# Two attention stages of a fused kernel: scores of two batches matmul by matmul on two halves of the rows, weighing in two parts

## The chip, the cores and the metric

The kernel runs as one program on one core of a Trainium2 chip. The time is device microseconds (us) of the execution, the median of several. The engines are named as in the profile: PE (TensorE, matmul), PEld (its weight loads), DVE (VectorE), ACT (ScalarE), POOL (GpSimd), SP (SyncE, here the issuer of most DMAs).

## The reference, cut to what matters

The program is a chain of eight layers on an input of 32 batches x 256 tokens x 128 features. Two of them are softmax attention with 16 heads of 8 features; everything else is untouched by the change.

```
# L2 attention (stage h2), causal
scores = einsum('bqhd,bkhd->bhqk', Q, K) / sqrt(8)
scores = where(causal, scores, -inf); attn = softmax(scores, -1)
out = einsum('bhqk,bkhd->bqhd', attn, V).reshape(...) @ W_o
# L3 attention inside the last FFN (stage h3), not causal, the same with biases
```

## The kernel before

`attend` runs twice: tag h2 with `causal=True`, tag h3 with `causal=False`. Both loop over 32 batches, in a hardware loop whose body is four batches (`SLOTS`), with three batches before it and four behind. Q and K arrive from DRAM as bf16 parts: 48 rows (`KR`, six parts of eight features) and 3 more (`KM` = 51) that hold, on the K side, ones and, on the Q side, first zeros and later the negated row maximum in three bf16 parts. The tiles `sq[u]` and `sk[u]` have 128 partitions x 16 heads x 256 tokens; partitions 51 to 127 are zero, and every score matmul contracts over all 128.

One pipelined `step(b, ...)` interleaves, head by head, three batches:

- `scores(b, u, h)` (L2105): K^T Q of head h of batch b, with the maximum already subtracted through the extra rows, into one of three PSUM banks (`ps_2`); two matmuls. ACT takes the exponential (`weights`, L2194) into `pt`.
- `max_scores(b + 2, ..., h)` (L2090): Q^T K of head h of the batch after the next, into one of two PSUM banks (`ps_1`); two matmuls. DVE takes its maximum (`maximum`, L2021) into `mx`.
- in h2 each of these matmuls is half or fully above the diagonal, so it has 128 or 256 columns, and is followed by a matmul of 128 columns that adds the mask (L2101, L2116).
- `weigh` (L2120), once for each group of four heads (`HG`): 8 matmuls in fp32 of V against `pt`, which write four column strips of 32 partitions; an fp32 matmul is two instructions for PE, so the trace has 16.
- around them: `turn_sums`, `turn_max`, `turn_out` (transposes) and `project_out`, on PE; `keep_sums` and the copies `oT`, `mpart` on ACT; `norm` (L2032: a reciprocal and a product), `mrest` (L2051), the residual add (L2056), `count` and `nm` (L2069) on DVE.

The order of all this is written out by hand in `step` of each engine: g runs over four groups, j over the four heads of a group. What waits for what is a semaphore count: `max_scores` of head h waits until DVE is done with head h - 2 (same bank), `scores` of head h until ACT is done with head h - 3. `project_out(b - 1)` stands on PE behind `scores` of head 12; it waits for ACT's copy `oT` (L2234), which stands on ACT behind `keep_sums` of the group and the exponential of head 11; and `keep_sums` waits for `weigh` (semaphore `pv`).

## Time and profile before

| | |
|---|---|
| median of 3 runs | 3908.71 us (3904.9 to 3912.76) |
| the profiled execution | 3900.78 us, its span 3898.9 us |
| mean granted clock of PE | 0.855 |
| busy | PE 2895.4 us (74%), DVE 2436.3 us (62%), ACT 1764.7 us (45%), POOL 594.0 us (15%) |
| first to last matmul of the scores of h2 and h3 | 1971 us to 2493 us, and 2977 us to 3507 us |

The profile is one execution. "Busy" is the time in which an engine had an instruction under way. A matmul's row lasts from its start to its result, so matmuls of a stream overlap: the pace is the distance of their starts. A row "x2, 0.39" is two matmuls merged. Idle time is shown in brackets with what ended it.

### The profile page before, as it was taken

To read this page: it belongs to the slowest core of one execution; us is meant where nothing else is said; L and a number is where in the kernel's file an instruction comes from. 1 tells how busy PE (TensorE), PEld (TensorE's weight loads), DVE (VectorE), ACT (ScalarE), POOL (GpSimd) and SP (SyncE) were. 2 spreads that over 40 slices of the span, in tenths; PEclk is the share of its full clock that TensorE was granted. 3 is DMA by queue.
4 is the path that set the end of the run, shared out by engine and by line. 5 is a ranking of instruction groups with operands and counts; after the bars stand their busy time and mean duration, and the time that the engine had idled before them with its cause. 6 is when DMAs were issued, how large, how long until landed. Compare 5 with 4: busy or idle time off the path is not lost. (4 is left out here: it accounts for less than half of the span.)

```text
span 3898.9 us, 82957 instructions
## 1 busy us (share of the span) xinstructions
PE 2895.4 (74%) x22031; PEld 2090.7 (54%) x22031; DVE 2436.3 (62%) x6570; ACT 1764.7 (45%) x4634; POOL 594.0 (15%) x911
## 2 busy tenths in 40 slices
PE   0444976999898688992469999868894999994061
PEld 0233563459787458991257777765452555554060
DVE  5852767238786435775667777557446777767167
ACT  5320632334353355661346666621122666672243
POOL 0000000000000586770000000000000000000773
PEclk9977968999997899996889999886556999995595
DMA  9069200100001111224865555000255555420123
GB/s 223 5 132 250 65 6 8 33 24 0 0 1 49 37 46 57 68 66 117 283 72 67 66 64 67 13 1 0 77 188 88 64 63 63 63 34 31 47 78 101
DMA packets 348796, 264.84 MB, mean 68 GB/s; under 512 B 20504, under 2 KB 331208, under 8 KB 348040
## 3 DMA queue, kind: packets, MB, share of 16 engines
q1 hardware_dynamic: 326944, 227.12, 29.0%
q0 software_dynamic: 12928, 26.70, 2.0%
q10 hardware_dynamic: 8704, 8.39, 0.7%
q8 instruction: 101, 1.65, 0.2%
q14 instruction: 119, 0.97, 0.1%
HBM read 145.70 MB, written 114.86 MB: 67 GB/s over the span
## 5 line engine op out<-in xcount | busy, mean ns | idle before, releaser
L2098 PE MATMUL h_ps<-h_sk,h_sq 128*128 128x256 bf16 (+1 forms) x2048 | 407.1, 267 | 113.1 <-DMA h_vb<-v_ones 95.9
L2113 PE MATMUL h_ps<-h_sq,h_sk 128*128 128x256 bf16 (+1 forms) x2048 | 393.9, 261 | 41.5 <-issue 21.2
L2030 DVE TENSOR_REDUCE h_mx<-h_ps 128x2 f32<-128x512 f32 x512 | 333.7, 684 | 114.7 <-PE h_ps L2098 96.7
L2204 ACT ACTIVATE h_pt<-h_ps 128x512 f32<-128x512 f32 x512 | 286.9, 593 | 100.1 <-PE h_ps L2113 89.7
L1446 POOL TENSOR_TENSOR idle<-idle 128x1 f32<-128x1 f32 x400 | 101.3, 253 | 1439.0 <-ACT e_row L1510 1368.4
L2098 PEld LDWEIGHTS h_ps<-h_sk,h_sq 128*128 128x128 bf16 x2048 | 174.7, 99 | 249.2 <-issue 120.3
L2201 ACT ACTIVATE h_pt<-h_ps 128x256 f32<-128x256 f32 x512 | 196.3, 383 | 115.3 <-PE h_ps L2116 113.4
L2128 PE MATMUL h_ps_o<-h_pt,h_vb 128*9 128x256 f32 (+1 forms) x4096 | 243.2, 355 | 0.9 <-ACT h_pt L2204 0.5
L2113 PEld LDWEIGHTS h_ps<-h_sq,h_sk 128*128 128x128 bf16 x2048 | 198.7, 99 | 77.8 <-issue 27.1
L1645 POOL DMA_INDIRECT results<-e_y,e_ykey x208 | 221.6, 1065 | 70.0 <-issue 67.0
L2080 POOL TENSOR_TENSOR h_mpart<-h_mrest,h_mpart 16x256 bf16<-16x256 f32 x64 | 42.3, 661 | 1242.7 <-ACT h_mpart L2230 1242.7
L2027 DVE TENSOR_REDUCE h_mx<-h_ps 128x1 f32<-128x128 f32 x512 | 147.2, 287 | 131.2 <-PE h_ps L2101 127.9
L2028 DVE TENSOR_REDUCE h_mx<-h_ps 128x1 f32<-128x256 f32 x512 | 211.6, 413 | 0.0
L1694 ACT ACTIVATE e_hid<-e_ps_h,e_wt 128x128 f32<-128x128 f32 x688 | 201.5, 367 | 7.4 <-PE e_ps_h L1668 3.0
L2101 PE MATMUL h_ps<-h_mskb 128*128 128x128 bf16 x1024 | 200.6, 222 | 0.0
L1603 DVE TENSOR_SCALAR e_wt<-w 128x1156 f32 (+1 forms) x208 | 142.8, 687 | 88.7 <-DVE e_y L1634 69.7
L1668 PE MATMUL e_ps_h<-e_hT,e_wt 128*128 128x128 f32 x1376 | 197.3, 283 | 0.3 <-ACT e_hT L1689 0.3
L1495 POOL DMA_INDIRECT sorted_rows<-e_row,e_key x192 | 189.3, 986 | 35.4 <-issue 18.8
L1676 PE MATMUL e_ps_o<-e_wt,e_hid 128*128 128x128 f32 x1376 | 190.0, 277 | 0.1
L1668 PEld LDWEIGHTS e_ps_h<-e_hT,e_wt 128*128 128x128 f32 x1376 | 174.2, 196 | 8.3 <-issue 2.3
L1661 PE MATMUL e_ps_t<-pack,e_xt 128*128 128x128 f32 x208 | 60.8, 294 | 158.7 <-DMA e_xt<-sorted_rows 158.3
L1676 PEld LDWEIGHTS e_ps_o<-e_wt,e_hid 128*128 128x128 f32 x1376 | 172.8, 194 | 0.4 <-issue 0.3
(410 smaller groups left out, 6878.9 us busy)
## 6 DMA issues: line engine op xcount, KB each, us to landing
h_sq<-q_stack SPq DMA_DIRECT2D x64, 384.0 KB
h_sk<-k_stack SPq DMA_DIRECT2D x64, 384.0 KB
sorted_rows<-pad SPq DMA_DIRECT2D x26, 520.0 KB, 10.5
e_xt<-sorted_rows SPq DMA_DIRECT2D x52, 260.0 KB, 2.8
e_got<-results SPq DMA_DIRECT2D x48, 256.0 KB, 4.6
q_stack<-p_parts SPq DMA_DIRECT2D x32, 384.0 KB, 2.6
k_stack<-p_parts SPq DMA_DIRECT2D x32, 384.0 KB, 3.3
v_ones<-p_v SPq DMA_DIRECT2D x32, 288.0 KB, 2.6
```

Source lines behind the costliest of these rows:

```text
L1645: gp.indirect_dma_start(ys[:, :], bass.IndirectOffsetOnAxis(ap=key[m // 4][:, m % 4:m % 4 + 1], axis=0), y[m % 4][:, :], None).then_inc(sc ...
L1668: pe.matmul(ps_h[:, k, 0:P], wt[j % 4][:, f * P:(f + 1) * P], hT[j % 4][:, :], start=True, stop=True).then_inc(e_h.sem, 1)
L1676: ins = pe.matmul(o, hid_t[m][:, f, :], wt[m][:, f_dim + f * D:f_dim + (f + 1) * D], start=(f == 0), stop=(f == nf - 1))
L1694: act.activation(hid_t[j % 4][:, f, :], ps_h[:, (j * nf + f) % 4, 0:P], func, bias=wt[j % 4][:, o_b1 + f:o_b1 + f + 1]).then_inc(e_a.sem, 1)
L2028: dve.tensor_reduce(mx[:, h, 1:2], sv[:, 1, :], AX, ALU.max).then_inc(s["mx"].sem, 1)
L2030: dve.tensor_reduce(mx[:, h, :], sv, AX, ALU.max).then_inc(s["mx"].sem, 1)
L2098: ins = pe.matmul(o, sq[u][:, h, q * P:(q + 1) * P], sk[u][:, h, 0:nk], start=True, stop=not causal)
L2101: ins = pe.matmul(o[:, q * P:nk], mskb[:, 0:P], mskb[:, P:2 * P], start=False, stop=True)
L2113: ins = pe.matmul(o[:, q0:], sk[u][:, h, t * P:(t + 1) * P], sq[u][:, h, q0:], start=True, stop=not causal)
L2128: ins = pe.matmul(o, vb[u][:, t, HG * g + j, :], pt[g % 2][:, j, t, q0:], start=(t == 0), stop=(t == TPB - 1), skip_group_check=True)
L2201: act.activation(to[:, 0, :], sv[:, 0, :], ACT.Exp, scale=scale)
L2204: act.activation(to, sv, ACT.Exp, scale=scale).then_inc(s["ex"].sem, 1)
```

## The change

Heads are split by parity. `sq` and `sk` have 8 places instead of 16; an even head lies on partitions 0 to 63 (51 used, the rest zeros), an odd head on 64 to 127. Each score matmul contracts over 64 partitions. On PE the two functions become one, `both(n)`, that waits for all it needs and then issues, in turn, matmul 0 of the scores of head n, matmul 0 of the maximum scores of head n ^ 1 (the other half of the partitions), matmul 1 and matmul 1. In h2 the four mask matmuls, which still contract over 128 partitions, come behind these four. DVE takes the maxima in the order 1, 0, 3, 2, ... `weigh` is issued in two parts, key tile 0 behind `both` of the third head of a group, key tile 1 behind that of the fourth; `turn_sums` moves ahead of `both` of the fourth head, `turn_max` behind the second part of `weigh`. DVE does `norm` behind the maximum of the fourth head, not ahead of it. Head 15 of the scores uses bank 1 instead of 0, so head 0 of the next batch needn't wait for it. Loads of a batch are 7 DMAs instead of 4 (half the size each, but for V), the maxima come in by 2 DMAs instead of 1.

The diff, with the unchanged part of long passages cut:

```diff
-                ("min", 16), ("s2", NH), ("ex", NH), ("pv", 4), ("ev", 4), ("tu", 4), ("rec", 4), ("on", 4), ("ot", 1),
+                ("min", 32), ("s2", NH), ("ex", NH), ("pv", 4), ("ev", 4), ("tu", 4), ("rec", 4), ("on", 4), ("ot", 1),
-            loaded=[SlotSignal(pool, f"{t}_loaded{u}", 64, u, 4) for u in range(4)]) for t in ("h2", "h3")}
+            loaded=[SlotSignal(pool, f"{t}_loaded{u}", 112, u, 4) for u in range(4)]) for t in ("h2", "h3")}
...
-                sq = [sb(f"{tag}_sq{u}", [P, NH, SEQ], BF16, stack=st) for u in range(SLOTS)]
-                sk = [sb(f"{tag}_sk{u}", [P, NH, SEQ], BF16, stack=st) for u in range(SLOTS)]
-                zrow = sb(f"{tag}_zrow", [KM - KR, NH, SEQ], BF16, stack=st)
+                sq = [sb(f"{tag}_sq{u}", [P, NH // 2, SEQ], BF16, stack=st) for u in range(SLOTS)]
+                sk = [sb(f"{tag}_sk{u}", [P, NH // 2, SEQ], BF16, stack=st) for u in range(SLOTS)]
+                zrow = sb(f"{tag}_zrow", [KM - KR, NH // 2, SEQ], BF16, stack=st)
...
+                def bank_of(h):
+
+                    return h % 3 if h < NH - 1 else 1
...
-                            sp.dma_start(sk[u][KR:KM, :, :], ones_rows).then_inc(ones_in[n_att], 16)
+                            for half in (0, 64):
+                                sp.dma_start(sk[u][half + KR:half + KM, :, :], ones_rows[:, 0:NH // 2, :]
+                                             ).then_inc(ones_in[n_att], 16)
...
-                            sp.dma_start(sq[u][0:KR, :, :], q_stack.rearrange("h e a t -> (e a) h t")[:, :, cols]
-                                         ).then_inc(up, 16)
-                            sp.dma_start(sk[u][0:KR, :, :], k_stack.rearrange("h e a t -> (e a) h t")[:, :, cols]
-                                         ).then_inc(up, 16)
-                            sp.dma_start(sq[u][KR:KM, :, :], zrow[:, :, :]).then_inc(up, 16)
+                            for odd in range(2):
+                                rows = slice(64 * odd, 64 * odd + KR)
+                                sp.dma_start(sq[u][rows, :, :], q_stack.rearrange("(h o) e a t -> o (e a) h t", o=2)
+                                             [odd, :, :, cols]).then_inc(up, 16)
+                                sp.dma_start(sq[u][64 * odd + KR:64 * odd + KM, :, :], zrow[:, :, :]).then_inc(up, 16)
+                                sp.dma_start(sk[u][rows, :, :], k_stack.rearrange("(h o) e a t -> o (e a) h t", o=2)
+                                             [odd, :, :, cols]).then_inc(up, 16)
...
-                                sp.dma_start(sq[ahead(u, r, 1)[0]][KR:KM, :, :], m_parts).then_inc(s["min"].sem, 16)
+                                for odd in range(2):
+                                    sp.dma_start(sq[ahead(u, r, 1)[0]][64 * odd + KR:64 * odd + KM, :, :],
+                                                 m_parts.rearrange("a (h o) t -> o a h t", o=2)[odd]
...
-                        def maximum(b, h):
-                            dve.wait_ge(*at("s1", b, h + 1))
-                            if h == 0:
+                        def maximum(b, n):
+                            h = n ^ 1
+                            dve.wait_ge(*at("s1", b, n + 1))
...
+                                    if first:
+                                        maximum(b + 2, HG * g + j)
                                     if j == 3 and g < 2 and tail:
                                         norm(b - 1, g + 2)
                                     if j == 3 and g >= 2 and body:
                                         norm(b, g - 2)
-                                    if first:
-                                        maximum(b + 2, HG * g + j)
...
-                        pe.wait_ge(ones_in[n_att], 16 * SLOTS)
-
-                        def max_scores(b, u, r, h):
...
-                        def weigh(b, u, g):
+                        pe.wait_ge(ones_in[n_att], 2 * 16 * SLOTS)
+
+                        def max_score(u, h, q):
+                            rows = slice(64 * (h % 2), 64 * (h % 2) + 64)
+                            nk = (q + 1) * P if causal else SEQ
+                            o = ps_1[:, h % 2, q * SEQ:q * SEQ + nk]
+
+                            return pe.matmul(o, sq[u][rows, h // 2, q * P:(q + 1) * P], sk[u][rows, h // 2, 0:nk],
+                                             start=(q == 0 or not causal), stop=not causal, skip_group_check=causal)
+
+                        def max_mask(h, q):
+                            o = ps_1[:, h % 2, q * SEQ + q * P:q * SEQ + (q + 1) * P]
+                            return pe.matmul(o, mskb[:, 0:P], mskb[:, P:2 * P], start=False, stop=True, skip_group_check=True)
+
+                        def score(u, h, t):
+                            rows = slice(64 * (h % 2), 64 * (h % 2) + 64)
+                            q0 = t * P if causal else 0
+                            o = ps_2[:, bank_of(h), t * SEQ:(t + 1) * SEQ]
+                            return pe.matmul(o[:, q0:], sk[u][rows, h // 2, t * P:(t + 1) * P], sq[u][rows, h // 2, q0:],
+                                             start=(t == 0 or not causal), stop=not causal, skip_group_check=causal)
+
+                        def score_mask(h, t):
+                            o = ps_2[:, bank_of(h), t * SEQ + t * P:t * SEQ + (t + 1) * P]
+                            return pe.matmul(o, mskb[:, 0:P], mskb[:, 2 * P:3 * P], start=False, stop=True, skip_group_check=True)
+
+                        def weigh(b, u, g, t):
 
                             pe.wait_ge(*at("ex", b, HG * (g + 1)))
                             pe.wait_ge(*at("ev", b, g))
-                            for t in range(TPB):
-                                q0 = t * P if causal else 0
-                                for j in range(HG):
-                                    o = ps_o[32 * j:32 * j + VW, 0, q0:SEQ]
-                                    ins = pe.matmul(o, vb[u][:, t, HG * g + j, :], pt[g % 2][:, j, t, q0:], start=(t == 0),
-                                                    stop=(t == TPB - 1), skip_group_check=True)
-                            ins.then_inc(s["pv"].sem, 1)
+                            q0 = t * P if causal else 0
+                            for j in range(HG):
+                                o = ps_o[32 * j:32 * j + VW, 0, q0:SEQ]
+                                ins = pe.matmul(o, vb[u][:, t, HG * g + j, :], pt[g % 2][:, j, t, q0:], start=(t == 0),
+                                                stop=(t == TPB - 1), skip_group_check=True)
+                            if t == TPB - 1:
+                                ins.then_inc(s["pv"].sem, 1)
...
-                            later = ahead(u, r, 2)
+                            later, r_later = ahead(u, r, 2)
+
+                            def both(n):
+
+                                if body:
+                                    if n == 0:
+                                        pe.wait_ge(*at("min", b, 32))
+                                    pe.wait_ge(*at("ex", b, n - 2 if 1 < n < NH - 1 else (-3, 0)[n] if n < 2 else n - 1))
+                                if first:
+                                    if n == 0:
+                                        pe.wait_ge(*s["loaded"][later].now(r_later, 112))
+                                    pe.wait_ge(*at("mx", b + 2, n - 1))
+                                for k in range(TPB):
+                                    if body:
+                                        ins = score(u, n, k)
+                                        if k == TPB - 1 and not causal:
+                                            ins.then_inc(s["s2"].sem, 1)
+                                    if first:
+                                        ins = max_score(later, n ^ 1, k)
+                                        if k == TPB - 1 and not causal:
+                                            ins.then_inc(s["s1"].sem, 1)
+                                if body and causal:
+                                    score_mask(n, 0)
+                                    score_mask(n, 1).then_inc(s["s2"].sem, 1)
+                                if first and causal:
+                                    max_mask(n ^ 1, 0)
+                                    max_mask(n ^ 1, 1).then_inc(s["s1"].sem, 1)
+
                             for g in range(GROUPS):
                                 for j in range(HG):
-                                    if body:
-                                        scores(b, u, HG * g + j)
+                                    if j == 3:
+                                        if g < 2 and tail:
+                                            turn_sums(b - 1, g + 2)
+                                        if g >= 2 and body:
+                                            turn_sums(b, g - 2)
+                                    both(HG * g + j)
                                     if j == 1 and g == 2 and tail:
                                         turn_out(b - 1, turn)
                                     if j == 0 and g == 3 and tail:
                                         project_out(b - 1)
-                                    if j == 2:
+                                    if j >= 2:
                                         if g and body:
-                                            weigh(b, u, g - 1)
+                                            weigh(b, u, g - 1, j - 2)
                                         if not g and tail:
-                                            weigh(b - 1, (u - 1) % SLOTS, GROUPS - 1)
-                                    if j == 3:
-                                        if g < 2 and tail:
-                                            turn_sums(b - 1, g + 2)
-                                        if g == 0 and turn:
-                                            turn_max(b + 1)
-                                        if g >= 2 and body:
-                                            turn_sums(b, g - 2)
-                                    if first:
-                                        max_scores(b + 2, *later, HG * g + j)
+                                            weigh(b - 1, (u - 1) % SLOTS, GROUPS - 1, j - 2)
+                                    if j == 3 and g == 0 and turn:
+                                        turn_max(b + 1)
...
-                            sv = ps_2[:, h % 3, :].rearrange("p (t q) -> p t q", t=TPB)
+                            sv = ps_2[:, bank_of(h), :].rearrange("p (t q) -> p t q", t=TPB)```

On PE in h3, around `project_out` (L2161 and L2162 of before, L2166 and L2167 of the change). Before, L2098 is the maximum, L2113 the scores, L2128 the weighing, L2136 `turn_sums`:

```order
L2128 MATMUL h_ps_o<-h_pt,h_vb 9x256 x8
L2094 REGISTER_ALU
L2098 MATMUL h_ps<-h_sk,h_sq 128x256 x2
L2109 REGISTER_ALU
L2113 MATMUL h_ps<-h_sq,h_sk 128x256 x2
L2134 REGISTER_ALU
L2136 MATMUL h_ps_s<-pack,h_sums 128x128 x2
L2094 REGISTER_ALU
L2098 MATMUL h_ps<-h_sk,h_sq 128x256 x2
L2109 REGISTER_ALU
L2113 MATMUL h_ps<-h_sq,h_sk 128x256 x2
L2157 REGISTER_ALU
```

With the change, L2118 is the scores, L2107 the maximum, L2132 the weighing, L2141 `turn_sums`:

```order
L2132 MATMUL h_ps_o<-h_pt,h_vb 9x256 x4
L2139 REGISTER_ALU
L2141 MATMUL h_ps_s<-pack,h_sums 128x128 x2
...
L2132 MATMUL h_ps_o<-h_pt,h_vb 9x256 x4
L2178 REGISTER_ALU
L2182 REGISTER_ALU
L2118 MATMUL h_ps<-h_sq,h_sk 128x256
L2107 MATMUL h_ps<-h_sk,h_sq 128x256
L2118 MATMUL h_ps<-h_sq,h_sk 128x256
L2107 MATMUL h_ps<-h_sk,h_sq 128x256
L2162 REGISTER_ALU
```

Between the end of the weighing and the wait of `project_out` (the last row) there were the maximum of two heads and the scores of two; now there is one `both`.

On PE in h2, one head before and one head with the change (L2101, L2116 and L2112, L2123 are masks):

```order
L2094 REGISTER_ALU
L2098 MATMUL h_ps<-h_sk,h_sq 128x128
L2101 MATMUL h_ps<-h_mskb 128x128
L2098 MATMUL h_ps<-h_sk,h_sq 128x256
L2101 MATMUL h_ps<-h_mskb 128x128
L2109 REGISTER_ALU
L2113 MATMUL h_ps<-h_sq,h_sk 128x256
L2116 MATMUL h_ps<-h_mskb 128x128
L2113 MATMUL h_ps<-h_sq,h_sk 128x128
L2116 MATMUL h_ps<-h_mskb 128x128
```

```order
L2182 REGISTER_ALU
L2118 MATMUL h_ps<-h_sq,h_sk 128x256
L2107 MATMUL h_ps<-h_sk,h_sq 128x128
L2118 MATMUL h_ps<-h_sq,h_sk 128x128
L2107 MATMUL h_ps<-h_sk,h_sq 128x256
L2123 MATMUL h_ps<-h_mskb 128x128 x2
L2112 MATMUL h_ps<-h_mskb 128x128 x2
```

The count of matmuls is the same; the masks moved from between to behind, so each head now goes once from matmuls on half the rows to matmuls on all of them and back.

## Rows read from the trace of the kernel before

**Rows 1.** Windows: PE, PEld, DVE, ACT, POOL busy us (count), clock, DMA share, GB/s.
```profile
2100.00:2200.00 100.00, 92.01 (x1296) 72.60 (x1296) 74.44 (x283) 68.74 (x244) 3.97 (x6) 0.99 0.49 65
3100.00:3200.00 100.00, 94.61 (x922) 57.00 (x922) 78.44 (x182) 69.70 (x145) 3.96 (x6) 1.00 0.53 66
```
**Rows 2.** Timeline of DVE, once a batch: start us, us; h2, then h3.
```profile
2246.41 0.18 DVE L2069 TENSOR_SCALAR h_nm<-h_mx 128x32 f32<-128x32 f32 x1
2261.58 0.17 DVE L2069 TENSOR_SCALAR h_nm<-h_mx 128x32 f32<-128x32 f32 x1
...
3193.46 0.18 DVE L2069 TENSOR_SCALAR h_nm<-h_mx 128x32 f32<-128x32 f32 x1
3209.57 0.18 DVE L2069 TENSOR_SCALAR h_nm<-h_mx 128x32 f32<-128x32 f32 x1
```
**Rows 3.** Timeline of PE in h2: the maximum scores of two heads in a row.
```profile
2252.34 0.22 PE L2098 MATMUL h_ps<-h_sk,h_sq 128*128 128x128 bf16 x1
...
2252.90 0.22 PE L2098 MATMUL h_ps<-h_sk,h_sq 128*128 128x128 bf16 x1
```
**Rows 4.** Timeline of PE in h2, around one weighing.
```profile
2250.64 0.22 PE L2116 MATMUL h_ps<-h_mskb 128*128 128x128 bf16 x1
2250.78 0.84 PE L2128 MATMUL h_ps_o<-h_pt,h_vb 128*9 128x256 f32 x16
2251.56 0.23 PE L2098 MATMUL h_ps<-h_sk,h_sq 128*128 128x128 bf16 x1
```
**Rows 5.** Timeline of PE in h3: a weighing, one head, sums turned.
```profile
3201.09 1.05 PE L2128 MATMUL h_ps_o<-h_pt,h_vb 128*9 128x256 f32 x16
3202.08 0.39 PE L2098 MATMUL h_ps<-h_sk,h_sq 128*128 128x256 bf16 x2
3202.31 0.38 PE L2113 MATMUL h_ps<-h_sq,h_sk 128*128 128x256 bf16 x2
3202.52 0.38 PE L2136 MATMUL h_ps_s<-pack,h_sums 128*128 128x128 f32 x2
```
**Rows 6.** Timeline of PE in h3: `project_out`, 1-row and 128-row matmuls in turn.
```profile
3203.65 0.48 PE L2161 MATMUL h_ps_m<-pack 1*128 1x128 f32 x2 [0.31 <-ACT h_oT L2234]
...
3204.28 0.28 PE L2162 MATMUL h_ps_m<-pack,h_oT 128*128 128x128 f32 x1
3204.48 0.37 PE L2161 MATMUL h_ps_m<-pack 1*128 1x128 f32 x1
```
**Rows 7.** Timeline of DVE and PE in h2: last mask of a maximum, and its reduction.
```profile
2251.79 0.22 PE L2101 MATMUL h_ps<-h_mskb 128*128 128x128 bf16 x1
2252.05 0.29 DVE L2027 TENSOR_REDUCE h_mx<-h_ps 128x1 f32<-128x128 f32 x1 [0.49 <-PE h_ps L2101]
2252.25 0.41 DVE L2028 TENSOR_REDUCE h_mx<-h_ps 128x1 f32<-128x256 f32 x1
```
**Rows 8.** Timeline of DVE in h3, and of PE where it waited for DVE.
```profile
3202.51 0.69 DVE L2030 TENSOR_REDUCE h_mx<-h_ps 128x2 f32<-128x512 f32 x1 [0.82 <-PE h_ps L2098]
...
3209.18 0.48 DVE L321 BATCH_NORM_STATS2 bn<-x  x2
...
3210.01 1.95 DVE L2030 TENSOR_REDUCE h_mx<-h_ps 128x2 f32<-128x512 f32 x3 [0.27 <-DVE h_nm L2069]
3211.88 0.20 DVE L2037 RECIPROCAL h_rec<-h_ps_s 128x8 f32<-128x8 f32 x1
...
3212.25 1.87 DVE L2030 TENSOR_REDUCE h_mx<-h_ps 128x2 f32<-128x512 f32 x3
3212.99 0.39 PE L2098 MATMUL h_ps<-h_sk,h_sq 128*128 128x256 bf16 x2 [0.23 <-DVE h_mx L2030]
```
**Rows 9.** Timeline of ACT in h3: the sums kept behind the weighing.
```profile
3202.29 0.38 ACT L2209 ACTIVATE h_sums<-h_ps_o 128x256 f32<-128x256 f32 x1 [0.49 <-PE h_ps_o L2128]
```
**Rows 10.** Timeline of PE in h2 where the hardware loop turns.
```profile
2262.78 0.28 PE L2113 MATMUL h_ps<-h_sq,h_sk 128*128 128x256 bf16 x1 [2.29 <-issue]
```
**Rows 11.** One line's instructions, min/median/max ns: the clearing of `sq`.
```profile
L2014 DVE MEMSET h_sq<- x8: 1765/1765/1765, 1938.9 to 2959.4; 128x2048 uint32 x8
```

More of the change, by code:

```diff
@@ L2003, in step @@
                                 sp.wait_ge(*at("mout", b + 1, 16))
-                                sp.dma_start(sq[ahead(u, r, 1)[0]][KR:KM, :, :], m_parts).then_inc(s["min"].sem, 16)
+                                for odd in range(2):
+                                    sp.dma_start(sq[ahead(u, r, 1)[0]][64 * odd + KR:64 * odd + KM, :, :],
+                                                 m_parts.rearrange("a (h o) t -> o a h t", o=2)[odd]
+                                                 ).then_inc(s["min"].sem, 16)
                         for b in range(SLOTS):
@@ L2087, in _ @@
                         pe.wait_ge(chained, k_set)
-                        pe.wait_ge(ones_in[n_att], 16 * SLOTS)
-                        def max_scores(b, u, r, h):
-                            if h == 0:
-                                pe.wait_ge(*s["loaded"][u].now(r, 64))
-                            pe.wait_ge(*at("mx", b, h - 1))
-                            for q in range(TPB):
-                                nk = (q + 1) * P if causal else SEQ
-                                o = ps_1[:, h % 2, q * SEQ:q * SEQ + nk]
-                                ins = pe.matmul(o, sq[u][:, h, q * P:(q + 1) * P], sk[u][:, h, 0:nk],
-                                                start=True, stop=not causal)
-                                if causal:
-                                    ins = pe.matmul(o[:, q * P:nk], mskb[:, 0:P], mskb[:, P:2 * P],
-                                                    start=False, stop=True)
-                            ins.then_inc(s["s1"].sem, 1)
@@ L2105, in scores @@
-                        def scores(b, u, h):
-                            if h == 0:
-                                pe.wait_ge(*at("min", b, 16))
-                            pe.wait_ge(*at("ex", b, h - 2 if h else 0))
-                            for t in range(TPB):
-                                q0 = t * P if causal else 0
-                                o = ps_2[:, h % 3, t * SEQ:(t + 1) * SEQ]
-                                ins = pe.matmul(o[:, q0:], sk[u][:, h, t * P:(t + 1) * P], sq[u][:, h, q0:],
-                                                start=True, stop=not causal)
-                                if causal:
-                                    ins = pe.matmul(o[:, q0:q0 + P], mskb[:, 0:P], mskb[:, 2 * P:3 * P],
-                                                    start=False, stop=True)
-                            ins.then_inc(s["s2"].sem, 1)
@@ L2122, in weigh @@
+                        def score_mask(h, t):
+                            o = ps_2[:, bank_of(h), t * SEQ + t * P:t * SEQ + (t + 1) * P]
+                            return pe.matmul(o, mskb[:, 0:P], mskb[:, 2 * P:3 * P], start=False, stop=True, skip_group_check=True)
+                        def weigh(b, u, g, t):
                             pe.wait_ge(*at("ex", b, HG * (g + 1)))
                             pe.wait_ge(*at("ev", b, g))
-                            for t in range(TPB):
-                                q0 = t * P if causal else 0
-                                for j in range(HG):
-                                    o = ps_o[32 * j:32 * j + VW, 0, q0:SEQ]
-                                    ins = pe.matmul(o, vb[u][:, t, HG * g + j, :], pt[g % 2][:, j, t, q0:], start=(t == 0),
-                                                    stop=(t == TPB - 1), skip_group_check=True)
@@ L2197, in weights @@
                             act.wait_ge(*at("pv", b, g - 1))
-                            sv = ps_2[:, h % 3, :].rearrange("p (t q) -> p t q", t=TPB)
+                            sv = ps_2[:, bank_of(h), :].rearrange("p (t q) -> p t q", t=TPB)
                             to = pt[g % 2][:, j]
```

1 line of the change is left out of this document (added).

## The prediction

> **What bounds the kernel now.** The kernel is a chain of layers, and the change touches two of them, so I read these two alone: the windows first, then the pace of a batch, then single instructions in time. In the windows [rows 1] PE is busy 92% in h2 and 95% in h3, DVE 74% and 78%, ACT below both, the clock is at its upper level of 2.4 GHz (0.99 and 1.00), DMA at half. The batch takes 15.2 us in h2 (2246.41 to 2261.58) and 16.1 us in h3 [rows 2]. So PE is the first suspect, in h2 above all: the maximum scores of a head begin 0.56 us behind those of the head before [rows 3], 16 x 0.56 = 9.0 of the 15.2 us; a weighing takes 2250.64 + 0.06 to 2251.56, 0.86 us [rows 4], four make 3.4; transposes and the output projection fill the rest. In h3 four score matmuls of 256 columns take 0.44 us (3202.08 to 3202.52) [rows 5], 7.0 us a batch; the rest of the 16.1 is weighing, projection and waits between PE and DVE, as the 0.82 us in which DVE stood still behind a weighing [rows 8].
>
> **What the change gives.** Two matmuls on different halves of the rows should run beside each other. That matmuls on different parts of the array do so this trace shows for column strips only: the 16 of a weighing, of 0.38 us each, start and stream within 0.99 us [rows 5]. Taken for row halves: in h3 a head costs PE 0.22 instead of 0.44 us (two streams of 256 columns), in h2 0.22 instead of 0.32 before masks (0.56 with them, at 0.06 for each mask). If nothing overlaps, both stay; that is the other end.
>
> **What it costs on PE: changes of shape.** Where PE goes from matmuls on all of the array to matmuls on a part, the trace has a gap. In h2 the last mask starts at 2250.64 and streams 0.06, the weighing starts at 2250.78: 0.08 lost [rows 4]. `project_out` of h3 has it for rows, not columns: behind a 128-row matmul at 3204.28 that streams 0.11 the 1-row matmul starts at 3204.48, 0.09 late, and its own row lasts 0.37 instead of 0.28 because its weights could not be loaded ahead [rows 6]. I take 0.10 for each change of shape, 0.15 into an fp32 transpose; the ends are 0 (if halves of 64 rows don't count as a shape of their own) and 0.20. The Trainium skill (TensorEngine Tiling, Key Properties) says that changing the tiling mode drains TensorE, while changing the tile within a mode doesn't; it gives no duration. The rows above agree; by that rule each `both` of h2 pays twice.
>
> In h2 a head then takes 0.22 + 0.10 + 4 x 0.055 + 0.10 = 0.64 us instead of 0.56. The overlap saves 0.10 and the two changes cost 0.20.
>
> **h2, one group of four heads.** Times from the start of `both` of its third head, each step from the durations above. `both` to 0.54; first half of the weighing 0.64 to 1.07 (four strips of two streams of 256 columns, 0.43); sums turned to 1.44; `both` of the fourth head 1.54 to 2.08; second half of the weighing 2.18 to 2.39 (128 columns); `both` of the next head 2.49 to 3.03. DVE starts 0.26 behind the last mask and works 0.61 [rows 7], so a maximum starts 0.75 behind its `both`: the fourth from 2.29 to 2.90. Then `norm`, now behind it: the reciprocal starts 0.08 before the end (1.95 us from 3210.01, reciprocal at 3211.88) and the next maximum 0.37 later [rows 8]: 3.19. The next maximum starts at 3.24 and ends at 3.85. PE needs 0.06 to go on behind DVE (second maximum of the 1.87 us from 3212.25 still runs; the first ends at 3212.93, PE at 3212.99) [rows 8]. So the third head of the next group starts at **3.91**. This is the new wait: before, `max_scores` alone waited for DVE and the scores of the next head ran meanwhile; now both wait, and the signal to DVE comes only behind four masks. Group 0 has `turn_max` as well (0.37): 4.28. The last group has `count` and `nm` behind `norm`, 0.83 from 3209.18 to 3210.01 [rows 8], which the slack of DVE hid before: 2.29 + 0.53 + 0.37 + 0.83 + 0.67 = 4.69.
>
> **`project_out`.** ACT's chain: end of the weighing, sums kept (3202.29 [rows 9]), exponential of head 11, copy `oT`, projection at 3203.65 [rows 6]. From the end of the weighing's streams (3202.08 - 0.10) that is 1.67 us. Before, PE had two heads' maxima and scores to do meanwhile and stood idle 0.31 [rows 6]. Now the weighing ends one `both` later and only one `both` lies between, so PE and, behind it, DVE stand. In h2: 2.39 + 1.67 = 4.06, projection 0.6 (four fp32 matmuls; half of h3's at most 0.8), next `both` 4.76 to 5.30, third head at 5.40. The batch: 4.28 + 3.91 + 5.40 + 4.69 = 18.3 instead of 15.2, **+3.1 us**; x 31 full batches = +96.
>
> **h3, the same.** Here DVE sets the pace: a maximum 0.62 behind the last ((1.87 - 0.68) / 2 is 0.60, (1.95 - 0.68) / 2 is 0.63) [rows 8], ready 0.45 behind `both` (3202.08 to 3202.51 for two matmuls 0.11 apart [rows 5, 8]). From the first maximum of a group at 0: `both` of the third head at 0.74, weighing half, sums turned, three gaps, `both` of the fourth at 0.74 + 0.22 + 0.10 + 0.43 + 0.10 + 0.27 + 0.10 = 1.96; its maximum at 2.41, 0.55 later than DVE could; `norm`; next group at 2.41 + 0.60 + 0.37 = 3.38. Group 0 has `turn_max`: 3.63. With the projection (1.6; half of it takes 3203.65 to 3204.48 [rows 6]): first maximum of the last group at 3.63 + 3.38 + 3.38 = 10.39, weighing ended at 9.72, projection 11.39 to 12.99, `both` of head 13 at 13.09, of 14 at 13.31, of 15 at 14.53, maximum 15 at 14.98, then 0.60 + 0.37 + 0.83: **16.8 instead of 16.1**, x 31 = +22. PE has 0.22 x 16 = 3.5 us less to stream in a batch; it goes into gaps (some 25 a batch, 2.5 us) and waits.
>
> **Smaller parts.** Eight clearings a stage at 1.765 us become half as long [rows 11], and so does that of `zrow`: 8 us ahead of all work of each stage, -16. At the turn of the hardware loop in h2 PE stands 2.29 us for "issue" [rows 10], once in four batches, 7 times; a PE that runs less far ahead of its waits hides part of it: -10, between 0 and -30. The DMAs: the same bytes in seven issues instead of four, 3 batches ahead; nothing waits there while a batch takes 15 us. Two DMAs for the maxima instead of one: some 0.3 us on a chain with microseconds to spare; nothing.
>
> **Sum.** +96 + 22 - 16 - 10 = +92. The profiled execution (span 3898.9, 3900.8 with what lies around) would go to 3993; the median lies 7.9 higher, so 3908.7 + 92 = **4000 us**.
>
> **Rivals.**
> *Halves of the rows change without a gap (faster).* For it: no row of this trace has a 64-row matmul. Against: rows 6. Then in h2 a head takes 0.44, a group 0.44 + 0.43 + 0.22, `both` at 1.09, its maximum at 1.74, the next at 2.64, third head at 3.31; with projection (1.74 + 1.67 + 0.6 = 4.01) 4.45, last 4.09: 15.2, nothing won or lost, since the wait for ACT and the delayed signal stay. In h3 `both` of the fourth at 1.61, group 3.04, last group as above: 15.5, -0.6 x 31 = -19. With -16 and -10: 3864. It decides from a gap below 0.03.
> *Halves do not overlap.* The Trainium skill (TensorE: Matmul & The Clock Gate, Part 3) has matmuls on different row groups start about 4 ns apart; no row here shows it. Without overlap each `both` takes 0.22 more in h3 and 0.10 in h2; two lie in the chain of each group: +1.8 and about +1 a batch, +87: 4087.
> *Half a gap*, 0.05: between the first rival and the forecast, 3930; with more of the waits hidden than I find, no change.
>
> **Chances.** Forecast (3945 to 4060) 0.60; no gap or waits that hide better 0.25; half a gap 0.08; no overlap 0.07. The range 3860 to 4060 holds the first three but for the tail of the second. Within 0.2% (3901 to 3916), which is about what a measurement of this kernel can tell from no change, I put 0.06; faster 0.25; slower 0.69.
>
> **What would show it.** In the profile after: the `nm` rows 18.3 us apart in h2 and 16.8 in h3 (step by step: below 15.2 in h2 and the forecast has failed); in h2 0.10 us between the last row matmul and the first mask beyond the stream, and again behind the masks; PE idle over 1 us ahead of the projection; DVE idle some 2 us behind it; score and maximum matmuls that start in pairs. Masks that follow without a gap would bring down the h2 term, pairs 0.11 us apart would raise both.

## Result and profile after

| | before | after |
|---|---|---|
| median of 4 runs each | 3906.81 us | 4041.5 us (4028.94 to 4045.2) |
| ratio, 95% interval | 1 | 1.0339 (1.0311 to 1.0367) |
| the profiled execution, its span | 3900.78, 3898.9 us | 4028.94, 4027.1 us |
| mean granted clock | 0.855 | 0.844 |

Slower by 3.4%, where the prediction said slower, 4000 us, at most 4060. The forecast was +92 us in a profiled execution; the two spans are 128.2 apart. The first and last start of the score matmuls say where. For each kernel the first row is h2 and the second h3. Before:

```profile
L2113 PE MATMUL h_ps<-h_sq,h_sk x1024: 217/272/421, 1993.8 to 2492.5; 128*128 128x256 bf16 x171
L2113 PE MATMUL h_ps<-h_sq,h_sk x1024: 269/273/421, 3000.3 to 3506.5; 128*128 128x256 bf16 x171
```

After:

```profile
L2118 PE MATMUL h_ps<-h_sq,h_sk x1024: 213/278/393, 1989.6 to 2579.0; 64*128 64x256 bf16 x171
L2118 PE MATMUL h_ps<-h_sq,h_sk x1024: 266/279/418, 3060.9 to 3633.6; 64*128 64x256 bf16 x171
L2025 DVE MEMSET h_sq<- x8: 912/912/912, 1943.3 to 3024.1; 128x1024 uint32 x8
```

h2 went from 498.7 to 589.4 (**+90.7**), h3 from 506.2 to 572.7 (**+66.5**); ahead of h2 -4.2, between the two stages 507.8 to 481.9 (-25.9), behind h3 +1.1. The last row is the halved clearing [rows 11]. From the first clearing to the first matmul of a maximum, a stage now takes 12 us less: 22.1 us instead of 34.5 ahead of h2 (1942.1 to 1964.2, and 1936.7 to 1971.2), and 22.2 instead of 33.8 ahead of h3. Ahead of h2 that is partly hidden, since the layers before it ended 5 us later. The other 14 between the stages lie in layers that the change does not touch.

Windows of after over both stages (columns as [rows 1]), then one batch of h3 at a lower clock, one at the full clock; last, for after and for before, what follows the last `nm` of h3:

```profile
2000.00:2520.00 520.00, 457.92 (x5762) 223.66 (x5760) 335.22 (x1245) 274.64 (x1081) 17.83 (x27) 0.97 0.35 55
3070.00:3590.00 520.00, 435.91 (x4292) 158.96 (x4295) 370.39 (x840) 301.68 (x669) 19.60 (x30) 0.90 0.35 55
...
3294.50:3314.00 19.50, 16.52 (x148) 5.46 (x148) 12.78 (x30) 10.02 (x24) 0.66 (x1) 0.82 0.33 52
3332.03:3348.65 16.62, 13.59 (x148) 5.22 (x148) 12.68 (x30) 10.47 (x25) 0.66 (x1) 1.00 0.40 61
...
3598.10:3633.60 35.50, 32.20 (x220) 10.46 (x220) 4.99 (x22) 19.29 (x43) 0.66 (x1) 0.67 0.01 3
3483.70:3506.50 22.80, 20.91 (x222) 11.57 (x211) 4.75 (x20) 18.35 (x42) 0.66 (x1) 1.00 0.02 5
```

PE is busy 88% in h2 and 84% in h3, where it was 92 and 95 [rows 1]. In h3 the clock is 0.90 where it was 1.00: a batch takes 16.62 us at the full clock (16.1 before [rows 2]) and mostly 17.5 to 19.6 where it fell; only about a third of the batches had it whole.

Timeline of PE in h2 after, one head and the projection:

```profile
2300.02 0.28 PE L2118 MATMUL h_ps<-h_sq,h_sk 64*128 64x256 bf16 x1
2300.02 0.34 PE L2107 MATMUL h_ps<-h_sk,h_sq 64*128 64x128 bf16 x2
2300.14 0.22 PE L2118 MATMUL h_ps<-h_sq,h_sk 64*128 64x128 bf16 x1
2300.29 0.28 PE L2123 MATMUL h_ps<-h_mskb 128*128 128x128 bf16 x2
2300.41 0.27 PE L2112 MATMUL h_ps<-h_mskb 128*128 128x128 bf16 x2
2301.39 0.71 PE L2167 MATMUL h_ps_m<-pack,h_oT 128*128 128x128 f32 x4 [0.70 <-ACT h_oT L2263]
```

The two streams of the two halves start together. The pair streams 384 columns on either half (0.16 us), the mask starts 0.27 behind: 0.11 lost at the change of shape. A head takes 0.60 us (2226.42 to 2227.02), 0.56 before [rows 3].

Timeline of PE, DVE and ACT in h3 after, a weighing in two parts and the projection:

```profile
3332.99 0.28 PE L2118 MATMUL h_ps<-h_sq,h_sk 64*128 64x256 bf16 x1 [0.35 <-DVE h_mx L2042]
3332.99 0.28 PE L2107 MATMUL h_ps<-h_sk,h_sq 64*128 64x256 bf16 x1
...
3333.11 0.27 PE L2107 MATMUL h_ps<-h_sk,h_sq 64*128 64x256 bf16 x1
3333.31 0.62 PE L2132 MATMUL h_ps_o<-h_pt,h_vb 128*9 128x256 f32 x8
3333.86 0.44 PE L2141 MATMUL h_ps_s<-pack,h_sums 128*128 128x128 f32 x2
3334.23 0.28 PE L2118 MATMUL h_ps<-h_sq,h_sk 64*128 64x256 bf16 x1
...
3343.59 0.48 PE L2166 MATMUL h_ps_m<-pack 1*128 1x128 f32 x2 [1.02 <-ACT h_oT L2263]
```

```profile
3334.69 0.69 DVE L2042 TENSOR_REDUCE h_mx<-h_ps 128x2 f32<-128x512 f32 x1 [0.55 <-PE h_ps L2107]
...
3345.72 0.69 DVE L2042 TENSOR_REDUCE h_mx<-h_ps 128x2 f32<-128x512 f32 x1 [2.20 <-PE h_ps L2107]
```

```profile
3345.68 1.08 ACT L2233 ACTIVATE h_pt<-h_ps 128x512 f32<-128x512 f32 x2 [1.66 <-PE h_ps L2118]
```

Those are the predicted waits: DVE 0.55 behind the first half of a weighing (0.24 in the group in which it also does `mrest`), PE 1.02 ahead of the projection (0.31 before [rows 6]), and behind the projection DVE 2.20 and ACT 1.66.

### The profile page after: what moved, and what is told of

Read it like the earlier page. It is cut to its first block and busy times, and to the rows that moved or that the text cites. A ratio compares the mean times of both kernels' runs of the same rounds, so it can differ in the third digit from the quotient of the medians.

```text
span 4027.1 us, 83705 instructions
## 1 busy us (share of the span) xinstructions
PE 2957.0 (73%) x22031; PEld 1858.7 (46%) x22031; DVE 2432.7 (60%) x6570; ACT 1708.8 (42%) x4634; POOL 594.4 (15%) x911
## 5 line engine op out<-in xcount | busy, mean ns | idle before, releaser
L2118 PE MATMUL h_ps<-h_sq,h_sk 64*128 64x256 bf16 (+1 forms) x2048 | 379.5, 276 | 99.8 <-DVE h_mx L2042 28.4
L2107 PE MATMUL h_ps<-h_sk,h_sq 64*128 64x256 bf16 (+1 forms) x2048 | 390.6, 281 | 73.3 <-DMA h_vb<-v_ones 69.2
L2042 DVE TENSOR_REDUCE h_mx<-h_ps 128x2 f32<-128x512 f32 x512 | 337.5, 685 | 161.8 <-PE h_ps L2107 142.9
L2132 PE MATMUL h_ps_o<-h_pt,h_vb 128*9 128x256 f32 (+1 forms) x4096 | 313.8, 381 | 1.9 <-ACT h_pt L2233 1.0
L2233 ACT ACTIVATE h_pt<-h_ps 128x512 f32<-128x512 f32 x512 | 280.9, 588 | 74.9 <-PE h_ps L2118 72.2
L2118 PEld LDWEIGHTS h_ps<-h_sq,h_sk 64*128 64x128 bf16 x2048 | 121.0, 96 | 318.5 <-issue 134.5
L2238 ACT ACTIVATE h_sums<-h_ps_o 128x256 f32<-128x256 f32 x256 | 98.1, 383 | 371.3 <-PE h_ps_o L2132 371.3
L2107 PEld LDWEIGHTS h_ps<-h_sk,h_sq 64*128 64x128 bf16 x2048 | 122.6, 97 | 97.4 <-issue 71.0
```

Source lines behind the costliest of these rows:

```text
L2042: dve.tensor_reduce(mx[:, h, :], sv, AX, ALU.max).then_inc(s["mx"].sem, 1)
L2107: return pe.matmul(o, sq[u][rows, h // 2, q * P:(q + 1) * P], sk[u][rows, h // 2, 0:nk], start=(q == 0 or not causal), stop=not causal, sk ...
L2118: return pe.matmul(o[:, q0:], sk[u][rows, h // 2, t * P:(t + 1) * P], sq[u][rows, h // 2, q0:], start=(t == 0 or not causal), stop=not cau ...
L2132: ins = pe.matmul(o, vb[u][:, t, HG * g + j, :], pt[g % 2][:, j, t, q0:], start=(t == 0), stop=(t == TPB - 1), skip_group_check=True)
L2233: act.activation(to, sv, ACT.Exp, scale=scale).then_inc(s["ex"].sem, 1)
```

## Experiments

Ratios are to the kernel before on the same chip; e9 to e11 ran on another, where before takes 3945.6 us (3903.1 and 3902.8 for the others). The extra time of that chip lies ahead of h2 (in e11 the first matmul of a maximum starts at 2025.9, before at 1971.2), so batches can be compared. The table gives the batch at the full clock, and clock and PE busy share in 2000:2450 (h2) and 3100:3450 (h3); where a stage starts later the window does too, 2050:2500 for h2 of e9 to e11 and 3435:3785 for h3 of e2. Below, "less than after" goes by the medians. By the ratios, each good to 0.2 to 0.4%, e3 lies 33 us under after, e4 40, e6 8 and e7 57, and e5 lies 21 over it; so e6 can't be told from after by its time.

| run | ratio (95%) | h2 batch, clock, busy | h3 batch, clock, busy |
|---|---|---|---|
| before | 1 | 15.1, 0.98, 93% | 16.1, 1.00, 95% |
| after | 1.0339 | 17.65, 0.97, 88% | 16.62, 0.89, 84% |
| e1_full_rows | 1.0394 (1.0355 to 1.0432) | 17.52, 0.98, 88% | 18.13, 0.96, 89% |
| e2_same_half | 1.1738 (1.1702 to 1.1775) | 19.6, 0.62, 97% | 18.4 to 18.8, 0.67, 92% |
| e3_mask_half | 1.0255 (1.0224 to 1.0286) | 15.40, 0.89, 79% | as after, 0.91, 84% |
| e4_project_later | 1.0237 (1.0201 to 1.0272) | 17.05, 0.97, 90% | 16.34, 0.94, 85% |
| e5_weigh_whole | 1.0393 (1.0349 to 1.0436) | 17.27, 0.96, 87% | 17.12, 0.88, 79% |
| e6_project_last | 1.0319 (1.0282 to 1.0356) | 16.97, 0.95, 91% | 16.35, 0.90, 84% |
| e7_last_and_mask_half | 1.0193 (1.0155 to 1.0231) | 15.4, 0.92, 79% | as e6, 0.91, 84% |
| e8_before_project_last | 0.9964 (0.9946 to 0.9982) | 15.1, 0.98, 92% | 15.83, 1.00, 95% |
| e9_joined_only | 1.0223 (1.0198 to 1.0248) | 16.2, 0.96, 89% | 17.31, 1.00, 89% |
| e10_split_only | 1.0186 (1.0163 to 1.0209) | 16.4, 0.99, 93% | 17.39, 1.00, 93% |
| e11_before_project_mid | 1.0029 (1.0011 to 1.0047) | 15.1, 0.98, 93% | 16.44, 1.00, 94% |

**What do the halves give, what does the order cost?** e1_full_rows is the change with full-row tiles and the four DMAs of before:

```diff
-                            rows = slice(64 * (h % 2), 64 * (h % 2) + 64)
+                            rows = slice(0, P)
```

> The changed kernel with its order of work, but the tiles, loads and score matmuls of before: all score and maximum matmuls contract over 128 partitions, so nothing overlaps and nothing changes shape but the weighing and the projection. Theory (the changes of shape cost 0.10 us each, the overlap gives 0.10 a head in h2 and 0.22 in h3, the order of work makes the waits): a head of h2 goes from 0.61 to about 0.55 us and the batch from 17.65 to 16.9 us; a batch of h3 from 16.6 at the upper clock to 17.5 or 18, with a steadier clock since PE streams more; in all 4020 to 4070 us, within 1% of the changed kernel, so still well above before: the order by itself is slower. Rival (the new order is harmless, the half rows do the damage): back to before but for the missing overlap, 3900 to 3930 us.

4057.28 us, as expected, though with 17.5 us a batch in h2 and not 16.9. At the full clock the new order alone costs 2.4 us a batch in h2 and 2.0 in h3. On top, the halves add 0.1 in h2 (overlap against two changes of shape) and take 1.5 off in h3. So on full rows the order alone costs as much in h2 as the whole change, where I had put more on the shapes; and what the halves save in h3 the clock gives back (0.96 to 0.89).

**Is the overlap real?** e2_same_half: the maximum scores of head n, on the same half as its scores.

```diff
-                                        ins = max_score(later, n ^ 1, k)
+                                        ins = max_score(later, n, k)
```

> The changed kernel with the maximum scores of head n beside the scores of head n, both on the same half of the partitions, instead of head n ^ 1 on the other: no two matmuls can overlap, everything else stays. Theory (halves overlap almost fully): the starts of score and maximum matmuls are no longer in pairs but 0.11 us apart, h3 gains 0.4 to 0.5 us in each group of four heads (+1.6 to +2 a batch), h2 +0.1 to 0.2 in each group; in all +60 to +90 us over the changed kernel, 4100 to 4130. Rival (the pairs in the trace are only records, the streams are serial in the array): within 10 us of the changed kernel.

4573.56 us (five runs, 4505.54 to 4584.14; the profile is the fastest), over 440 beyond both expectations. Timeline of PE in h2, with its row behind a turn of the hardware loop; then windows: short ones at either clock, one batch at the full clock, and the whole stretch at the lower one:

```profile
2114.79 0.28 PE L2118 MATMUL h_ps<-h_sq,h_sk 64*128 64x256 bf16 x1
2114.91 0.22 PE L2107 MATMUL h_ps<-h_sk,h_sq 64*128 64x128 bf16 x1
2114.96 0.22 PE L2118 MATMUL h_ps<-h_sq,h_sk 64*128 64x128 bf16 x1
2115.02 0.27 PE L2107 MATMUL h_ps<-h_sk,h_sq 64*128 64x256 bf16 x1
...
2129.11 0.28 PE L2118 MATMUL h_ps<-h_sq,h_sk 64*128 64x256 bf16 x1 [3.07 <-issue]
```

```profile
2112.00:2117.00 5.00, 5.00 (x59) 2.86 (x58) 3.31 (x14) 2.95 (x13) 0.00 (x0) 1.00 0.77 137
2132.00:2157.00 25.00, 24.99 (x170) 11.92 (x167) 9.62 (x34) 8.55 (x32) 0.66 (x1) 0.50 0.26 42
...
2107.60:2127.20 19.60, 17.81 (x200) 9.77 (x200) 12.40 (x47) 9.94 (x39) 0.66 (x1) 1.00 0.35 54
2130.40:2212.10 81.70, 81.60 (x542) 39.05 (x542) 33.01 (x117) 27.52 (x103) 1.98 (x3) 0.50 0.24 38
```

On one half the matmuls follow one another (0.12, 0.05, 0.06 us apart), so the overlap of after is real. At the full clock a batch of h3 takes 18.4 to 18.8 us, 1.8 to 2.2 over after, as expected; one of h2 takes 19.6, 2.0 over after instead of 0.4 to 0.8. What was not foreseen is the clock. It falls behind the 3.07 us in which PE stands at the turn of the hardware loop, and then stays at 0.50, the 1.2 GHz level, for 82 us in which PE was busy all but 0.1 us. In after, too, the clock of h2 falls behind the turns (23.1 us a batch at 0.85), but there it comes back within the batch.

**What do the changes of shape cost in h2?** e3_mask_half puts the masks on the half of their head: 64 rows, each row of the weights serving two neighbouring queries or keys by factors of 1 and 2^-80 against -2^40 and -2^120. In h2 then only the weighing and the transposes change the shape.

```diff
-                            return pe.matmul(o, mskb[:, 0:P], mskb[:, P:2 * P], start=False, stop=True, skip_group_check=True)
+                            rows = slice(64 * (h % 2), 64 * (h % 2) + 64)
+                            return pe.matmul(o, mskb[rows, 0:P], mskb[rows, P:2 * P], start=False, stop=True, skip_group_check=True)
```

> The changed kernel with causal masks that contract over the 64 partitions of their head's half (each row of the mask matmul serves two tokens, with weights 1 and 2^-80 against -2^40 and -2^120), issued in pairs like the scores: no change of shape within a head, and masks that overlap too. Theory (two changes of shape at 0.10 us in each head are the loss in h2): a head of h2 takes 0.35 to 0.40 us instead of 0.61, the batch about 16.0 instead of 17.65 us, in all 45 to 60 us less than the changed kernel, 3980 to 3995; h3 is untouched. Rival (h2 is slower because both kinds of scores now wait for both engines, PE's own time hardly matters): less than 15 us.

3996.45 us, 45 less than after. PE in h2:

```profile
2265.06 0.28 PE L2119 MATMUL h_ps<-h_sq,h_sk 64*128 64x256 bf16 x1
...
2265.24 0.22 PE L2113 MATMUL h_ps<-h_mskb 64*128 64x128 bf16 x1
2265.24 0.22 PE L2125 MATMUL h_ps<-h_mskb 64*128 64x128 bf16 x1
...
2265.54 0.28 PE L2119 MATMUL h_ps<-h_sq,h_sk 64*128 64x256 bf16 x1
```

The mask follows 0.18 behind instead of 0.27, and two masks run beside each other. So the edit takes two things off a head, two changes of shape (0.22) and half of the masks' streams (0.11), and no run parts them. At the full clock the batch takes 15.4 us (16.0 expected), 2.2 less than after, which would be 70 us; but most batches took 16 to 19 us, at a clock of 0.89 (0.97 in after).

**The waits around projection and weighing.** e4_project_later has the projection one head later (`j == 1`), e5_weigh_whole both parts of the weighing behind the third head, e6_project_last the projection and DVE's add at the step's end, e7_last_and_mask_half is e6 with e3's masks.

```diff
-                                    if j == 0 and g == 3 and tail:
+                                    if j == 1 and g == 3 and tail:
```

> The changed kernel with the output projection one head later on PE (behind head 13, not 12). Theory (PE stands because ACT's copy oT comes 1.67 us behind the weighing): the idle time before the projection falls from 1.02 us in h3 and 0.70 in h2 by one head's work, 0.3 and 0.6; DVE gets one more maximum to do, but the projection itself, 1.6 us in h3, still stands in DVE's way: 0.25 us a batch less in h3, 0.5 in h2, in all 15 to 30 us less. Rival (the projection's place doesn't matter, PE has slack there): within 5 us.

> The changed kernel with both parts of a weighing behind the third head of a group, as before the change, everything else as changed. Theory (two chains: DVE waits for the work between two heads' matmuls, ACT's copy oT waits for the end of the weighing): the fourth head's maximum comes 0.3 to 0.4 us later in each group, but ACT's chain starts 1.2 us earlier, so PE's idle time before the projection (1.02 us in h3, 0.70 in h2) goes; the two about cancel, within 20 us of the changed kernel. Rival (splitting the weighing is the main loss of the new order, through its extra change of shape and the late signal to ACT): 50 us or more less.

> The changed kernel with the output projection at the very end of a step on PE (behind the last part of the weighing of the last group), and on DVE the residual add and its statistics behind nm, at the end as well. Theory (the wait for oT and the projection itself in front of head 13 are a main part of the new order's loss): PE's idle time before the projection and the 2.20 us in which DVE stands there go, but the residual add now waits for the projection at the end: about 1.1 us a batch less in h3 and 0.9 in h2, 55 to 70 us less than the changed kernel, 3970 to 3990. Rival (it is only moved): within 20 us of the kernel with the projection one head later, 3975 to 4010, with DVE idle as long at the step's end.

> The projection at the end of the step and the causal masks on half the partitions, together. Theory (both terms are paths of their own, so they add: 45 for the masks, 55 to 70 for the projection): 3920 to 3945 us. Rival (the clock takes it back: with masks on halves the granted clock in h2 fell from 0.97 to about 0.89, and a batch takes 15.4 us at the upper level but up to 18.9 below it): 3960 or more, with a lower clock still in h2.

e4: 50 us less, where 15 to 30 were expected. At the full clock a batch lost 0.6 and 0.3 us, as expected (27 us in all); the rest goes with the clock of h3, 0.94 instead of 0.89. e5: 18 us slower than after, within the expectation: weighing whole is 0.4 us better in h2 and 0.5 worse in h3. e6: only 20 less, not 55 to 70, outside both expectations. The wait was moved, not removed: DVE's add now waits for the projection at the end (1.09 us in h3), and PE behind it for DVE (1.79). e7: 68 less, which is the rival's time (3960 or more), but not its reason: at the full clock h2 takes 15.4 us (15.1 before the change), and the clocks of 0.92 and 0.91 take part of the gain back, yet the clock of h2 is higher than in e3 (0.89), where the rival had it lower.

**The order, one part at a time.** From the kernel before: e9_joined_only has `both`, the turned pairs of maxima and `norm` behind the maximum, with full rows and a whole weighing (head 15 stays on bank 1); e10_split_only has the weighing in two parts and nothing else:

```diff
-                                    if j == 2:
+                                    if j >= 2:
                                         if g and body:
-                                            weigh(b, u, g - 1)
+                                            weigh(b, u, g - 1, j - 2)
```

> The kernel before with only the two functions joined: scores and maximum scores of a head wait together and are issued in turn (full rows, masks behind; DVE does norm behind the maximum); weighing whole, transposes where they were. Theory (the joint wait and the later signal to DVE are the main loss: with the whole new order on full rows a batch takes 17.5 us instead of 15.1 in h2 and 18.1 instead of 16.1 in h3): at least 1.2 us a batch in each stage, 3980 to 4040 us. Rival (the split weighing and the moved transposes are the loss): within 25 us of before.

> The kernel before with only the weighing in two parts, the second behind the scores of the fourth head. Theory (small part): DVE's wait behind the weighing shrinks by some 0.4 us in h3, ACT's chain to the projection starts one head later, one more change of shape pair in each group (0.2 us in h2, which is bound by PE): h2 +0.8 us a batch, h3 within 0.3 us, in all +10 to +35 us, 3915 to 3940. Rival (it is the main loss of the new order): 3980 or more.

+2.2% and +1.9%; together about e1's 3.9%. Each costs 1.1 to 1.3 us a batch in both stages, so the joined wait is no worse than the split, which I had expected at +10 to +35 us and measured at +72. That holds on full rows; with the whole new order on half rows, e5, the split costs 0.4 us a batch in h2 and saves 0.5 in h3. In h3 of e9 the matmuls of a head wait 29.5 us for DVE's maxima in 3100:3450, before 5.4. DVE in e10, h3:

```profile
3203.36 0.21 DVE L2037 RECIPROCAL h_rec<-h_ps_s 128x8 f32<-128x8 f32 x1 [0.54 <-PE h_ps_s L2136]
```

`norm` waits for sums that are turned behind the second part, once a group, ahead of the next maximum; before the change it hardly ever waited. Four times 0.53 are 2.1 us, more than the whole 1.3, since the waits for maxima get shorter: over 3100:3450 they go from 70.1 to 42.8 us, and 42.4 us of waiting for sums are new.

**A better version.** e8_before_project_last does to the kernel before what e6 did to after; e11_before_project_mid moves the projection one head only.

```diff
-                                    if j == 0 and g == 3 and tail:
+                                    if j == 3 and g == 3 and tail:
                                         project_out(b - 1)
```

> The kernel before with nothing changed but the place of the output projection (end of the step on PE) and of the residual add with its statistics (behind nm on DVE). Theory (there too DVE stands 1.38 us and ACT 1.77 us while PE waits for oT and projects, in h3): 0.3 to 0.8 us a batch less in h3, 0.2 in h2, 15 to 30 us less than before, 3875 to 3890. Rival (PE bounds it: 95% busy, the same work in another place): within 5 us of before.

> The kernel before with only the output projection moved, on PE, from behind the scores of head 12 to behind the maximum scores of head 13; DVE's residual add stays ahead of the maximum of head 14. Theory (PE then never waits for oT, and DVE has two maxima to do while PE projects, so its 1.38 us of standing go, and the add doesn't have to wait at the end of the step): as much as with the projection at the end of the step or a little more, 3875 to 3893 us. Rival (the gain at the step's end came from PE filling its own idle time, 0.3 us a batch, and there is no more to win): 3891 within 5 us.

e8: 3891.6 against 3902.83 us, ratio 0.9964 (0.9946 to 0.9982), ten runs against thirteen: the fastest kernel of this study, 3.6% faster than after by the two ratios. It falls just short of the 3875 to 3890 expected. h3 takes 15.83 us a batch instead of 16.10, which is 8 of the 11 us. e11 is slower than before by 0.3%, against both expectations: h3 16.44 (+0.34 a batch, times 31 is 10.5; the medians differ by 8.1). DVE in e11, then in e8, h3:

```profile
3200.75 0.42 DVE L2056 TENSOR_TENSOR x<-x,h_ps_m 128x256 f32 x1 [1.09 <-PE h_ps_m L2162]
...
3210.92 0.42 DVE L2067 TENSOR_TENSOR x<-x,h_ps_m 128x256 f32 x1 [0.47 <-PE h_ps_m L2161]
```

DVE's add waits 1.09 us for the projection, which the expectation had left out; before the change it did not wait. That is more than the maxima save: all of DVE's waits for PE in 3100:3450 go from 3.2 to 3.6 us a batch (70.1 in 21.7 batches, 52.1 and 23.9 in 21.3), about the 0.34. At the end of the step (e8) the add waits 0.47.

## Why the prediction came out as it did

- **h2, +96 less 10: measured +90.7.** The chain of a group was forecast at 3.91 us and is 3.88 (weighing to weighing, 2218.67 to 2222.55), the group with the projection at 5.40 and is 5.07; the batch 18.3, measured 17.65 to 18.0. A head was 0.64 and is 0.60, because the two streams of a pair take 0.16 and not 0.22; the change of shape was 0.10 and is 0.11. The Trainium skill (TensorEngine Tiling, Key Properties) says that a change of tiling mode drains TensorE; the rows agree. e3, whose masks keep the mode and overlap besides, is 2.2 us a batch faster. The first rival (no gap) is out; its 15.2 us for h2 left out the 0.37 of `turn_max`.
- **Turns of the hardware loop, -10: nothing.** Before, a batch with a turn took 19.5 us on average (six batches), 4.4 over the others; after, 22.4, 4.6 over. I took the idle time for one that later waits hide; but PE stands longer for it, 3.0 to 3.2 us where it was 2.2 to 2.5 and in most turns another 1.3 to 2.1 a little later, and the clock falls behind it.
- **h3, +22: measured +66.5, the step that failed.** The part that I worked out holds: 16.62 instead of 16.10 at the full clock (forecast 16.8), times 31 is +16, with DVE's stall of 0.55 in two of the groups to the hundredth. Of the other 50 us some 46 are the clock, which the sum left at 1.00 without a reason. Behind the second `nm` thirty batches took 536.7 us, 38 more than thirty at 16.62. The end of the stage, behind the last `nm`, took 35.5 us at a clock of 0.67, where e1, in the same order, takes 27.4 at 1.00 and before 22.8; so 8 of these us are clock and 4.6 the order. With full rows h3 keeps 1.00 under either half of the new order (e9, e10) and 0.96 under both (e1); every kernel with half rows there has 0.88 to 0.94, and e2, where they don't overlap, 0.67. So the half rows are needed for most of the fall. Half rows in the old order were not run, and what in the half rows does it is not shown.
- **Clearings, -16:** 12 us less in each stage from the first clearing to the first matmul of a maximum, -24. The direction is right, the gain half as large again as forecast.
- **Not in the sum:** -14 between the stages, from the last score matmul of h2 to the first clearing for h3, in work that the change doesn't touch. Windows of that stretch in before, after and e11:

```profile
2492.50:2943.60 451.10, 365.83 (x1408) 249.33 (x1406) 241.95 (x662) 112.02 (x188) 9.86 (x16) 0.64 0.21 67
2579.00:3015.70 436.70, 353.46 (x1414) 241.31 (x1412) 241.54 (x661) 111.69 (x188) 9.86 (x16) 0.66 0.21 69
2546.20:2984.60 438.40, 350.50 (x1408) 241.06 (x1406) 241.67 (x662) 112.03 (x188) 9.90 (x16) 0.67 0.21 69
```

  e11, which is the kernel before with one call moved, has it short as well. In the thirteen profiles the stretch takes 435 to 451 us, the longest in before, so the 14 us need no effect of the change.
- **No overlap** (second rival) is out by e2, **the joined wait and the late signal** cost what e9 shows (together; no run parts them), and the split what e10 shows. The price of h2 holds for half rows, not for the order as such: with full rows and no gaps (e1) h2 loses almost as much, since there the four streams of a head stand in a row.

The range (to 4060) held the time, 4041.5, with part of the change priced at less than half: h3 came out 44 us too low, and h2 with the turns 5. Luck took some of it back, the 14 us in other layers and 8 more from the clearings. Without both the time would have been about 4064, just outside.

## What to carry to other kernels

Halves of the array are worth having only where matmuls of that shape follow one another: price 0.1 us for each change of shape, and put what comes between (masks) on the same shape first. Before joining two waits or splitting a step that signals, write down who is signalled later: here, on full rows, each of the two cost 2%, more than the overlap gave. And count what faster, thinner matmuls do to the granted clock, since it can take back what they save; read the clock batch by batch, at the full clock the order's own effect shows.

## What was not expected of the hardware

- The clock does not follow the busy share of PE in the profile. e2 held PE busy 97% of 2000:2450 at a clock of 0.62, e1, with the same order, full rows and 88%, had 0.98. Part of the 97% comes from the low clock itself, at which each row is longer; but in batches at the full clock the two are alike, 91% (17.81 of 19.60 us) and 90% (15.79 of 17.60, in 2200.30:2217.90 of e1). The Trainium skill (TensorE: Matmul & The Clock Gate, What's actually happening) says the gate is set by how busy the PE has been recently; by the profile's busy rows that does not agree here. In h2 after, where the masks still use all rows, the clock is 0.97, hardly under e1's; with the masks on halves as well (e3) it is 0.89.
- Two streams on different row halves start within 0.01 us of one another and slow each other in nothing that the rows show: the eight 256-column matmuls of two heads, four on either half, start at 3345.26, 3345.38, 3345.49 and 3345.60, so the pace on a half is 0.11 us, as it is for one stream alone [rows 5]. That makes 0.23 us a head instead of 0.44.
- Moving the projection by one head or by three (e11, e8) changes the sign of its effect, with DVE's wait for it 1.09 and 0.47 us.
